# Graph network kernel, count stage: 16-bit item offsets, and the register load of a set placed between the items and the last two old-count matmuls of the set before

## The reference

```python
x = x + _L0_gnn_ref(h, qW, kW, vW, src, dst)                 # attention over the edges, 4 heads
x = x + _L1_gnn_ref(h, p_t, Wv, bv, edge_weight, edge_index) # softmax of edge weights by target
x = x + _L2_gnn_ref(h, src, dst, W, b)                       # sum over edges, then a linear map
x = x + _L3_gnn_ref(h, edge_index, w2, ..., bn_beta)         # Chebyshev terms, gate, batch norm
```

## Time and profile before

| | us |
|---|---|
| median of 3 runs | 1339.63 |
| lowest and highest | 1333.62, 1341.48 |
| span of the profiled execution | 1334.5 |
| count loop in it, first item matmul to last copy | 30.6 to 360.1, or 329.5 |
| busy over the whole span: PE, DVE, ACT, POOL | 1089.8, 974.4, 691.7, 599.0 |

### The profile page before, as it was taken

One profiled execution on the slowest core, in us unless ns is written; L12 is line 12 of the kernel. 1 busy time (PEld: TensorE's weight loads), 2 busy tenths in 40 slices (PEclk: granted clock), 3 DMA queues, 4 the chain that ended last, 5 costly groups with the idle time before them and its releaser, 6 DMA issues.

```text
span 1334.5 us, 23321 instructions
## 1 busy us (share of the span) xinstructions
PE 1089.8 (82%) x8345; PEld 633.6 (47%) x8345; DVE 974.4 (73%) x1600; ACT 691.7 (52%) x903; POOL 599.0 (45%) x343
## 2 busy tenths in 40 slices
PE   3878787787796888888788888837996999999893
PEld 2555554454461222222222222214696987788783
DVE  8677888886575999999999999918556535422466
ACT  7555565555446998999898999800000000000221
POOL 8532533422005998999999989960000000000000
PEclk9888878879796999999999999968997999999996
DMA  0100000000144111111112222110011000000201
GB/s 10 30 33 5 7 7 5 8 17 1 40 129 114 36 44 45 47 48 44 45 35 60 53 51 49 45 44 1 1 37 39 25 14 1 22 14 4 66 28 36
DMA packets 98907, 44.80 MB, mean 34 GB/s; under 512 B 85196, under 2 KB 96716, under 8 KB 98672
## 3 DMA queue, kind: packets, MB, share of 16 engines
q1 hardware_dynamic: 97104, 41.58, 11.8%
q0 software_dynamic: 1696, 1.74, 0.5%
HBM read 30.73 MB, written 12.56 MB: 32 GB/s over the span
## 4 chain that ended last, share of the span: by engine, by line
PE 50%; DVE 25%; issue 11%; ACT 5%; POOL 5%; DMA 2%; another core or an unknown queue 2%; SPq 1%; DVEq 0%; ACTq 0%; POOLq 0%
PE PS L1324 19%; DVE Eb L1150 15%; PE PS L553 10%; PE PS L557 8%; POOL Eb L982 3%; DVE Eb L1144 3%; PE PS L1709 3%; PE PS L1332 2%; ACT Eb L1115 2%; PE PS L1074 2%; PE PS L1064 1%; PE PS L1315 1%; ACT Eb L1117 1%; ACT Eb L1119 1%
## 5 line engine op out<-in xcount | busy, mean ns | idle before, releaser
L982 POOL TENSOR_SCALAR Eb<-Eb 128x1024 f32<-128x1024 f32 (+4 forms) x175 | 431.1, 2485 | 74.1 <-ACT Eb L1119 72.8
L1150 DVE SCALAR_TENSOR_TENSOR Eb<-Eb,PS 128x1024 f32<-128x1024 f32 (+4 forms) x350 | 366.7, 1084 | 16.7 <-ACT Eb L1117 10.5
L1324 PE MATMUL PS<-hs,CT 128*128 128x192 f16 (+3 forms) x2500 | 263.3, 267 | 4.0 <-DVE B L1557 1.8
L1119 ACT ACTIVATE Eb<-PS,small 128x1024 f32<-128x1024 f32 (+2 forms) x263 | 251.5, 997 | 28.0 <-PE PS L1064 24.5
L593 ACT ACTIVATE CT<-PS 128x500 f32 x313 | 183.7, 587 | 142.9 <-PE PS L557 135.1
L553 PE MATMUL PS<-mov,oneS 128*128 128x100 f16 x1565 | 184.6, 231 | 76.1 <-issue 71.0
L1324 PEld LDWEIGHTS PS<-hs,CT 128*128 128x128 f16 (+1 forms) x2500 | 227.5, 99 | 37.7 <-DVE SG L1557 2.7
L553 PEld LDWEIGHTS PS<-mov,oneS 128*128 128x128 f16 x1565 | 146.6, 107 | 157.9 <-issue 113.8
L1064 PE MATMUL PS<-Qb,Kb 96*128 96x512 f16 (+3 forms) x700 | 182.8, 364 | 11.1 <-ACT Eb L1119 7.2
L1074 PE MATMUL PS<-Eb,V 128*25 128x512 f32 (+3 forms) x1400 | 169.9, 558 | 3.4 <-DVE Eb L1150 1.8
L435 DVE TENSOR_TENSOR oneS<-iotaX,KL 128x2560 f16<-128x2560 int16 x80 | 120.1, 1501 | 71.6 <-PE PS L557 69.0
(11 more groups left out here) (258 smaller groups left out, 1006.6 us busy)
## 6 DMA issues: line engine op xcount, KB each, us to landing
Kb<-kd SPq DMA_DIRECT2D x168, 96.0 KB, 2.4
qd<-QH SPq DMA_DIRECT2D x12, 192.0 KB, 2.7
kd<-QH SPq DMA_DIRECT2D x12, 192.0 KB, 3.1
hs<-t_d SPq DMA_DIRECT2D x12, 192.0 KB, 2.5
Qb<-qd SPq DMA_DIRECT2D x4, 384.0 KB, 3.9
CT<-x_d SPq DMA_DIRECT2D x1, 1200.0 KB, 7.6
x_d<-B SPq DMA_DIRECT2D x6, 192.0 KB, 1.9
t_d<-A SPq DMA_DIRECT2D x6, 192.0 KB, 1.8
```

The source lines that it names most:

```text
L982: g.tensor_scalar(e, e, ELO, None, ALU.max).then_inc(S("floored"), 1)
L1119: a.activation(e, ps, ACT.Exp, scale=K.unsc[0:r, :]).then_inc(S("score_read"), 1)
L1150: v.scalar_tensor_tensor(out=e, in0=e, scalar=EHI, in1=cn, op0=ALU.min, op1=ALU.mult).then_inc(S("weighed"), 1)
L1324: m = p.matmul(bank(t % FIRST)[0:r, 0:w], K.CT[:, a, 128 * t:128 * t + r], hs[:, a, :, :].rearrange("p k d -> p (k d)"), start=(a == 0), s ...
```

## The change

The tables `wI` become 16-bit, with the 20 words of a set in a row of 24, and a second 16-bit table `wG` holds the four words of a set that ScalarE needs, in a row of 8; VectorE writes it with one more small copy for each of the three parts, behind a semaphore of its own (`base_set`). On PE the loop goes by sets: groups 0 and 1 as before, then the ten items of groups 2 and 3, then the register load of the next set, then the old-count matmuls of groups 2 and 3.

```diff
--- before.py
+++ after.py
@@ -141,7 +141,8 @@
     K.key = sb(st, "key", [128, CH], F32)
     K.va = sb(st, "va", [128, CH], F32)
     K.lo = sb(st, "lo", [128, 2, CH], F32)
-    K.wI = [sb(st, "wI%d" % h, [b - a, BLOCK], I32) for h, (a, b) in enumerate(PARTS)]
+    K.wI = [sb(st, "wI%d" % h, [b - a, 6, 24], I16) for h, (a, b) in enumerate(PARTS)]
+    K.wG = [sb(st, "wG%d" % h, [b - a, 6, 8], I16) for h, (a, b) in enumerate(PARTS)]
     K.turnW = sb(st, "turnW", [BLOCK, BLOCK], F32)
     K.win = sb(st, "win", [BLOCK, NJ], F32)
     K.cI = sb(st, "cI", [BLOCK, NJ], I32)
@@ -411,7 +412,10 @@
     def table(h):
 
         v.wait_ge(S("windows"), h + 1)
-        v.tensor_copy(K.wI[h][:, :], K.bank(4)[0:PARTS[h][1] - PARTS[h][0], 128:128 + BLOCK]).then_inc(S("reg_set"), 1)
+        table = K.bank(4)[0:PARTS[h][1] - PARTS[h][0], 128:128 + BLOCK]
+        v.tensor_copy(K.wI[h][:, :, 0:SET], table.rearrange("p (s k) -> p s k", k=SET)).then_inc(S("reg_set"), 1)
+        v.tensor_copy(K.wG[h][:, :, 0:4], table.rearrange("p (s g k) -> p s g k", g=4, k=GI)[:, :, :, 0]
+                      ).then_inc(S("base_set"), 1)
 
     for t in range(7):
         passes(0, t)
@@ -476,18 +480,21 @@
     v.wait_ge(step, own.n)
 
 
-def load_windows(K, e, ety, s, every):
-
-    j, o = s // 6, SET * (s % 6)
-    h = 0 if j == 0 else 1 if j < PARTS[2][0] else 2
-    r = j - PARTS[h][0]
-    e.wait_ge(K.S("reg_set"), h + 1)
+def load_windows(K, ety, words):
+
     _, vals = K.nc.values_load_multi_w_load_instructions(
-        K.wI[h][r:r + 1, o:o + SET:every], engines=[ety], min_val=0, max_val=W * (NW - 3),
+        words, engines=[ety], min_val=0, max_val=W * (NW - 3),
         skip_runtime_bounds_check_because="a window's first destination by the staircase")
-    n = SET // 4 // every
+    n = len(vals) // 4
     return [[x if k == 0 else x.with_bounds(min_val=0, max_val=(GI - 1) * W) for k, x in enumerate(vals[n * r:n * r + n])]
             for r in range(4)]
+
+
+def table_row(s):
+
+    j = s // 6
+    h = 0 if j == 0 else 1 if j < PARTS[2][0] else 2
+    return h, j - PARTS[h][0], s % 6
 
 
 def build_tensor(t, K):
@@ -510,6 +517,7 @@
         t.wait_ge(S("slot_w"), h + 1)
         if h:
             t.wait_ge(S("reg_set"), h)
+            t.wait_ge(S("base_set"), h)
         t.matmul(bank(4)[0:b - a, 128:128 + BLOCK], K.win[:, a:b], K.turnW[:, :], start=True, stop=True
                  ).then_inc(S("windows"), 1)
 
@@ -540,31 +548,52 @@
     t.wait_ge(S("zero_g"), 2)
     t.wait_ge(S("zero_v"), 1)
     t.wait_ge(S("zero_a"), 2)
-    for g in PRESENT:
-        s, o = g // 4, GI * (g % 4)
-        if g % 4 == 0:
-            words = vals = to = None
-            words = load_windows(K, t, mybir.EngineType.PE, s, 1)
-            t.wait_ge(S("one_hot"), s + 1)
-        vals = words[g % 4]
-        ps = bank(g % 4)[:, 0:25 * GI * W].rearrange("p (a c) -> p a c", a=25)
+
+    def group_bank(g):
+        return bank(g % 4)[:, 0:25 * GI * W].rearrange("p (a c) -> p a c", a=25)
+
+    def load(s):
+        h, r, o = table_row(s)
+        t.wait_ge(S("reg_set"), h + 1)
+        return load_windows(K, mybir.EngineType.PE, K.wI[h][r:r + 1, o, 0:SET])
+
+    def items(g, vals):
+        s, o, ps = g // 4, GI * (g % 4), group_bank(g)
         for k in range(GI):
             to = ps[:, :, 0:W] if k == 0 else ps[:, :, bass.ds(vals[k], W)]
             t.matmul(to, K.oneS[:, s % DEEP, o + k, :], K.mov[:, s % DEEP, o + k, :].rearrange("p (a w) -> p a w", a=25),
                      start=(k == 0), stop=False, skip_group_check=True)
+
+    def add_old(g, vals):
         if g >= 2:
             t.wait_ge(S("placed"), INDEX[g - 2] + 1)
-        t.matmul(ps, K.identb[:, :], K.CT[:, :, bass.ds(vals[0], GI * W)], start=False, stop=True, skip_group_check=True
-                 ).then_inc(S("counted"), 1)
-        if g == PRESENT[-1] or g // 4 != PRESENT[INDEX[g] + 1] // 4:
-            if s == SUM_AT:
-                sums(2)
-            if s == SLOTS_AT:
-                windows(2)
-            if s in TURN_AT:
-                turn_items(TURN_AT[s])
-            if SOFT_AT.get(s) in SOFT_TURN:
-                soft_turn(*SOFT_TURN[SOFT_AT[s]])
+        t.matmul(group_bank(g), K.identb[:, :], K.CT[:, :, bass.ds(vals[0], GI * W)], start=False, stop=True,
+                 skip_group_check=True).then_inc(S("counted"), 1)
+
+    words = load(0)
+    for s in range(SETS):
+        t.wait_ge(S("one_hot"), s + 1)
+        groups = [g for g in range(4 * s, 4 * s + 4) if g in INDEX]
+        for g in groups[:2]:
+            items(g, words[g % 4])
+            add_old(g, words[g % 4])
+        for g in groups[2:]:
+            items(g, words[g % 4])
+        left = [(g, words[g % 4][0:1]) for g in groups[2:]]
+        words = None
+        if s + 1 < SETS:
+            words = load(s + 1)
+        for g, vals in left:
+            add_old(g, vals)
+        left = vals = None
+        if s == SUM_AT:
+            sums(2)
+        if s == SLOTS_AT:
+            windows(2)
+        if s in TURN_AT:
+            turn_items(TURN_AT[s])
+        if SOFT_AT.get(s) in SOFT_TURN:
+            soft_turn(*SOFT_TURN[SOFT_AT[s]])
     t.wait_ge(S("counted"), len(PRESENT))
 
 
@@ -588,7 +617,9 @@
     for i, g in enumerate(PRESENT):
         s = g // 4
         if g % 4 == 0:
-            words = load_windows(K, a, mybir.EngineType.Activation, s, GI)
+            h, r, o = table_row(s)
+            a.wait_ge(S("base_set"), h + 1)
+            words = load_windows(K, mybir.EngineType.Activation, K.wG[h][r:r + 1, o, 0:4])
         a.wait_ge(S("counted"), i + 1)
         a.activation(K.CT[:, :, bass.ds(words[g % 4][0], GI * W)],
                      K.bank(g % 4)[:, 0:25 * GI * W].rearrange("p (a c) -> p a c", a=25), ACT.Copy).then_inc(S("placed"), 1)
```

## The result

The changed kernel takes 1651.7 us (median of 4 runs, 1647.9 to 1654.2) against 1339.0 for the kernel before: a ratio of 1.233, with a 95% interval of 1.230 to 1.237, or +313 us. The forecast was +16.

What follows compares the result with a forecast made beforehand. The prediction took PE's sequencer, with its uncovered register loads, to bound the count loop. Order +28 us and width -12 gave +16 on 1339.6, a forecast of 1356 us, range 1320 to 1372.

Steps and rivals of the forecast that it cites:

- The bound: Count loop: PE's sequencer ends last, each of 80 register loads takes 1.36 us, and nothing covers what a load loses.
- The width: PE's register load with 16-bit words: 1.21 us in place of 1.36, -12 us over 80 sets.
- a second step of the same size: Upper bound of PE's load, if each short word needs another step: 1.94 us.
- my three signs of being wrong: Load under 1.0 us, PE's matmuls running over 0.2 us into it at full clock, or no wait for the copy.
- The sentence on the rule of the Trainium skill: PE's load: 200 ns per register would make twenty words 4 us; the trace, with 1.36, disagrees.
- the load stays: PE's load priced by register, not byte: it remains 1.36 us and the change ends at +28 us.
- short words are dearer: Rival at PE's register load: 1.94 us a load, +74 us, 1414 us in all; chance 0.06.
- The order: Count loop: next set's first old-count matmul waits for ScalarE's copy; +0.42 us a set at full clock, +0.17 at half, +28.
- The marks: Expected profile after: PE idle for "issue" before the old-count matmul, and 20 to 30 us waiting for ScalarE's copy.
- Small parts: ScalarE's shorter or equal load, VectorE's three extra casts and its smaller cover: taken at 0 us.
- The sum: Whole kernel: +28 us for the order and -12 for the width make +16 us.
- the queue that hides the load: Rival: all ten items handed over before PE works on them, hiding part of the load; -21 us, 1318 us; chance 0.07.

Runs made afterwards that it cites:

- e3_width: The kernel before with only the tables made 16-bit, read by PE and ScalarE in the old order: 1627.2 us, ratio 1.216.
- e1_order: The changed kernel with its tables kept in 32-bit words, so the new order alone: 1374.1 us against 1339.6 for the kernel before, ratio 1.027.
- e8_order_act: The changed kernel's order with both tables in 32-bit words, ScalarE's load being one aligned read: 1361.1 us against 1328.0 for the kernel before, ratio 1.024.
- e2_one_left: New order with 32-bit tables, but only one old-count matmul (group 3's) behind the load: 1353.8 us against 1328.1 for the kernel before, ratio 1.021.
- m1_probe: The kernel before plus twelve register loads of various widths, counts and distances on SyncE's idle sequencer: 1337.3 us (one run).
- m2_probe: The kernel before plus twelve other register loads on SyncE's idle sequencer, varying first byte and word count: 1331.1 us.
- e7_one_left_act: New order, 32-bit tables including ScalarE's four words, one old-count matmul behind the load: 1331.3 us against 1328.0 for the kernel before, ratio 1.003.
- b6_pairs: The kernel before with 16-bit offsets loaded as aligned 32-bit pairs and split in the register steps; ScalarE has its own 32-bit table: 1335.7 us, ratio 1.008.
- b5_one_word: The kernel before with each group's offsets packed into one 32-bit word, fields taken out in the register steps: 1359.7 us against 1328.1, ratio 1.026.

## Why the prediction was wrong

- **The bound: right.** PE's sequencer ends last, and nothing covers the load: 269 us added to the loads in `e3_width` gave +288.
- **The width: the step that failed.** I took PE's 1.36 and ScalarE's 0.89 as two points of one line, a fixed 0.78 and 0.029 a word, and bounded the new load by that line's word at 0.78 and 1.94. They were two kinds of load: five reads of four words, and four reads of one. The slope between them meant nothing, and the upper bound, "a second step of the same size", inherited it. The load that I forecast at 1.21 measured 4.72, outside both bounds, because it is twenty reads of one word; at the forecast's own 8 us for 0.1 it is +269 in place of -12. None of my three signs of being wrong covered a load above the range.
- **The sentence on the rule of the Trainium skill ("Runtime: NRT & Kernel Launch", section "Instruction fetch mechanics") failed with it.** I said that the trace disagreed, from PE's row alone. ScalarE's row, 0.89 for four, is 0.22 a word and agreed. A rule that one row refutes and another confirms says that the rows differ in kind. An estimate by that rule, twenty words at 200 ns, is 4 us and makes the change +240: the nearest of all readings, and I had used of it only the part "the load stays". The rival "short words are dearer" had the right place and sign, at 1414 us and 0.06.
- **The order: right in mechanism, +28 forecast, +34.5 measured** (32 to 39 by the ratio). At the full clock the links were 0.50, 0.59 and 0.13 against the forecast's 0.50, 0.59 and 0.14, and a set grew by 0.45 (4.02 to 4.47) against 0.42. Two terms were too small. At the half clock a set grew by 0.28 (4.39 to 4.67) against 0.17. And more sets are at the half clock: the granted clock over the loop of `e1_order` is 0.75, not 0.85, so half of the time and not 0.30.

```profile
30.60:393.50 362.90, 257.44 (x1963) 167.90 (x1963) 254.89 (x242) 179.84 (x327) 114.94 (x114) 0.75 0.04 11
```

- **The marks.** Idle time of PE in front of the old-count matmul for "issue" came as said (83.2 us in `e1_order`, 332.0 in the changed kernel). The wait for the copy is 18.0 us in `e1_order` where 20 to 30 were said. In the changed kernel it shows as 0.9, no more than before: at the half clock PE is still streaming items (253.63 to 254.25) while its sequencer waits for the copy of group 2 (253.54 and 0.59), so PE shows no idle time. There the set is 8.01 - 4.72 = 3.29 us beside its load, where I had 3.18.
- **Small parts.** ScalarE's load costs nothing that could be measured in the new order, as said (`e8_order_act`, +33 against +34.5). In the next variant, one left behind, it cost some 20 us; my expectation for `e2_one_left` had followed only one chain.
- **The sum.** 269 for the loads and 34.5 for the order leave 9 of 313. `e3_width` needs some 19 beside its loads; on top of it the new order adds 24.5, less than 34.5. That fits the set lengths, since at the half clock, where the dear load puts most sets, the order costs less; no run isolates this share of the clock.
- **A slip in a rival.** For the queue that hides the load I wrote -0.4 a set at the half clock. 0.17 less 0.83 is -0.66, or -0.47 if the 0.19 already counted is taken off; it moves that rival by 2 to 6 us and changes nothing else.

## What to carry to other kernels

Count a register load by its reads, not by its bytes: keep the table in 32-bit words, start each load at a multiple of 16 bytes, and load in fours. With a narrower type each word is a read: four times the reads, here 4.72 us in place of 1.36. Before drawing a line through two rows of the trace, ask whether they differ in more than the one size: here alignment, distance and width all changed the kind. And when work is moved across a sequencer's wait, follow the buffers' readers on every engine, its own register loads too; which of them becomes the link depends on how many are left behind.

## What the runs showed of the hardware

- A register load has a fixed 0.3 us on SyncE and 0.20 to 0.23 us per read (`m1_probe`, `m2_probe`). On PE, 0.33, 0.85 and 1.36 for one, three and five reads give 0.26 a read and 0.07 fixed, and 4.72 and 7.08 for twenty and thirty single words give 0.24 a read. ScalarE was seen at two points only, 0.31 for one read and 0.89 for four. The Trainium skill, "DMA: Bandwidth & Descriptors", section "Latency and other measured facts", has a floor near 600 ns for `tensor_load`; the runs show 0.31 us, on ScalarE in `e7_one_left_act`.
- The register step of an item costs 0.037 us more with one shift or remainder written into it (0.046 to 0.083, `b6_pairs`), and 0.084 more with a shift, a remainder and a multiplication (0.130, `b5_one_word`).
- In the changed kernel PE stood still for 4.3 us of each 8.0; the loop's granted clock was 0.61, and 77 of 79 sets ran at the half clock (1.2 GHz). Before, PE idled 1.05 us in front of a set's first item, the granted clock was 0.85, and 19 sets ran at the half clock throughout.
